# Perceiver cross-attention on one core: value-side context blocks turned by DMA, probability sums on VectorE

## The chip, the cores and the metric

One Trainium2 chip, one core of it. The time is device microseconds of one execution of the whole program. Engines are named as in the profile: PE (TensorE), DVE (VectorE), ACT (ScalarE), POOL (GpSimd), SP (the queue that issues the DMAs).

## The reference, cut to what matters

The program computes one layer: cross-attention of 128 query rows on 12544 context rows, then a chunk of linear attention and a feed-forward block with ternary weights. Nearly all the time, and the whole change, is in the cross-attention.

```python
q = (inputs_q @ Wq).reshape(b, sq, H, HD) * (1.0 / np.sqrt(HD))     # 128 x 16 heads x 128
k = (inputs_kv @ Wk).reshape(b, skv, H, HD)                         # 12544 context rows of 512
v = (inputs_kv @ Wv).reshape(b, skv, H, HD)
scores = jnp.einsum('bqhd,bkhd->bhqk', q, k)
attn = jax.nn.softmax(scores, axis=-1)
ctx = jnp.einsum('bhqk,bkhd->bqhd', attn, v).reshape(b, sq, H * HD)
return ctx @ Wo
```

## The kernel before

**Absorbed weights.** Keys and values are never formed. For each head the query is multiplied by Wk, so that scores are products of a 128x512 query with the context itself; the weighted sum of context rows is multiplied by Wv and Wo at the end.

**Pairs of heads and a Strassen form.** Two heads and two halves of a context block make a 2x2 block product, which is done with seven products (Winograd's form). Operands therefore come in seven blocks, three or four given ones and four sums: A11, A12, A22, S1 to S4 for queries and probabilities, B11, B21, B22, T1 to T4 for the context. Each operand is split into a high and a low float16 part, and three of the four cross products are taken (`product` L1207, `value_product` L1218).

**Steps.** The context is 49 blocks of 256 rows. One step (`make_steps` L49, 136 of them) takes one pair of heads and a window of three neighbouring blocks (128 score columns for each block and head; narrower windows at either end). Eight pairs take turns while the window moves, so a block enters the ring about every 2.8 steps. The ring has 4 slots.

**Two copies of each block.** `make_loads` (L71) orders two loads for each block: kind 0, transposed (features on partitions, in `bulk`, moved through the scores), and kind 1, natural (rows on partitions, in `nring`, moved through the values). Each is four DMAs into the single buffer `stage` (L448, L452), four sums by POOL (`sum_t`, L561), a high part by ACT (`split_hi`, L629 or L632) and a low part by DVE (`split_lo`, L857 or L861). In steps 8 to 130 about three steps in four carry one of them. The transposed ring is laid out so that almost every window is one access pattern; slots 0 and half pieces interleave (`PLACES`, `window` L93). In windows {0,1,2} and {1,2,3} the columns come in another order, so that an exponential is made of two instructions for each head (`split_exp`, L648 and L651), otherwise of one (L655).

**A step on each engine**, in the order of its own queue:
- PE (`step`, `values`): seven score products, six matmuls each (L1214), into four PSUM regions; the last waits for `d_done` from DVE. Then the seven value products of the step two before it (L1227; `LAG` is 2): V1, V5, V6 and its neighbour, V7, V3, and the last, which waits for `vd_done`, the value sum of DVE. 42 score and 63 value matmuls for a full window.
- ACT: copies of partial scores (L686, L690, L692), the split if any, exponential of head 0 (L655 or L648 and L651), copy of V1 (L672), exponential of head 1, copies of V5 and V6 (L677, L681), two alphas (L711), then the high parts of the probabilities (L666): blocks A22, A11, A12 in one, then S1, S3, S2, S4.
- POOL: the four context sums if any, then the four sums of probabilities (`sum_p`, L580).
- DVE: maximum of head 0 (L874), adding and maximum (L869) twice, running row sums (L903, L905), the negated maxima (L881, L883), the split if any, in steps 50 to 112 every second time a quantisation of feed-forward weights (L935, L937, L941), the value sum (`value_sum_d`, L924), five low parts (L892), another value sum (L929), two accumulations (L914).
- SP: for the step before, two DMA transposes of the probabilities from `pp` to `pt` (24 and 18 tiles of 128x128, L462), then context loads, query weights (first steps), feed-forward weights.

An all-reduce over partitions on POOL (L591) stands in step 43, between its sums.

Of the kernel before, what the change touches and what calls it, by code (L numbers as in the profile page):

```python
# [5 lines left out]
P = 128  # L6
D = 512
KC = D // P
# [19 lines left out]
HALF = P // 2  # L28
PLACES = ((0, 1), (2, 5), (3, 4), (6, 7))
TW = P * RING  # L30
# [40 lines left out]
def make_loads():  # L71

    order = sorted([(user(c, False), 0, c) for c in range(NCH)] + [(user(c, False) + LAG, 1, c) for c in range(NCH)])
    loads, at = [], -1
    for need, kind, c in order:
        free = user(c - RING, True) + 1 + LAG * kind if c >= RING else -1
        at = max(free, min(at + 1, need - 1)) if c >= 1 else -1
        assert at < need, (kind, c, free, at, need)  # L80
        loads.append((kind, c, at))
    return loads


LOADS = make_loads()
LOAD_OF = {(kind, c): j for j, (kind, c, _) in enumerate(LOADS)}

# [5 lines left out]
def window(k):  # L93


    _, a, w = STEPS[k]
    slots = {ring_slot(c) for c in range(a, a + w)}
    return {
        frozenset((0, 1, 2)): (0, 6 * HALF, 1, 6 * HALF, (1, 0, 2), 0),
        frozenset((1, 2, 3)): (2 * HALF, 6 * HALF, 1, 6 * HALF, (1, 2, 3), HALF),  # L100
        frozenset((0, 2, 3)): (0, 3 * HALF, 3, 2 * HALF, (0, 2, 3), None),
        frozenset((0, 1, 3)): (0, 5 * HALF, 2, 3 * HALF, (0, 1, 3), None),
        frozenset((0, 3)): (0, 6 * HALF, 2, 2 * HALF, (0, 3), None),
        frozenset((2, 3)): (3 * HALF, 3 * HALF, 2, 2 * HALF, (2, 3), None),
        frozenset((0,)): (0, 2 * HALF, 1, 2 * HALF, (0,), None),
        frozenset((1,)): (2 * HALF, 3 * HALF, 2, HALF, (1,), None),
        frozenset((2,)): (3 * HALF, 2 * HALF, 1, 2 * HALF, (2,), None),
        frozenset((3,)): (6 * HALF, 2 * HALF, 1, 2 * HALF, (3,), None),
    }[frozenset(slots)]


def perceiver_layer(nc, x_d, ctx_d, qk_d, vo_d, aw_d, wg1_d, wg2_d, w12_d, ld_d, normw_d, b1_d,
                    lng_d, lnb_d, b2_d, ident_d, diff_d, mask_d, out_d):
    es = ExitStack()
    with es:
# [30 lines left out]
        rsum = sb("rsum", 2 * H)  # L146
# [44 lines left out]
        PURE = 4  # L191
# [7 lines left out]
        def runs(t, at, stride, n, m):  # L199

            if n == 1:
                return t[:, at:at + m]
            return t[:, at:at + n * stride].rearrange("p (n s) -> p n s", s=stride)[:, :, 0:m]

        def t_moving(k, lo, blk, c):
            start, stride, n, m, _, _ = window(k)
            return runs(bulk16, ((lo * 7 + blk) * 2 + c) * TW + start, stride, n, m)

# [4 lines left out]
        def n_part(c, lo, blk=0, n=1):  # L213
            at = ((ring_slot(c) * 2 + lo) * 7 + blk) * BLK
            return nring16[:, at:at + n * BLK]
# [16 lines left out]
        def bank_a(k):  # L232
            return ps_s[:, D - cols(k):D]

        def bank_e(k):
            return ps_s[:, D:D + cols(k)]
# [29 lines left out]
        in_ctx = sem("in_ctx")  # L266
        in_pt = [sem(f"in_pt{g}") for g in range(2)]
# [106 lines left out]
        def prep_at(k):  # L374

            for j, (kind, c, at) in enumerate(LOADS):
                if at == k:
                    return j, kind, c
            return None

        def t_ring(c, lo):

            a, b = PLACES[ring_slot(c)]
            ring = bulk16[:, lo * 14 * TW:(lo + 1) * 14 * TW].rearrange("p (b w) -> p b w", w=TW)
            if b == a + 1:
                return [ring[:, :, a * HALF:(a + 2) * HALF]]
            return [ring[:, :, a * HALF:(a + 1) * HALF], ring[:, :, b * HALF:(b + 1) * HALF]]

        def t_stage(j, n):

            blocks = stage[:, 0:7 * BLK].rearrange("p (b w) -> p b w", w=P)
            return [blocks[:, :, i * P // n:(i + 1) * P // n] for i in range(n)]
# [8 lines left out]
        def pp_part(k, lo, blk, n=1):  # L401
            at = p_at(k, blk // PURE, lo, blk % PURE)
# [6 lines left out]
        A21 = -1  # L409

        def prob_of(k, g):
            return prob_part(k, (A21, A11)[g], 2)

# [7 lines left out]

        def split_exp(k):
            return window(k)[5] is not None
# [12 lines left out]
        def _(sp):  # L436
# [5 lines left out]
            def load_ctx(j):  # L442
                kind, c, _ = LOADS[j]
                if j:
                    sp.wait_ge(ctx_lo, j)
                if kind == 0:
                    for n, blk in enumerate((B11, B12, B21, B22)):
                        sp.dma_start(stage[:, blk * BLK:(blk + 1) * BLK].rearrange("p (c n) -> p c n", c=2),  # L448
                                     ctx_d[4 * c + n // 2].rearrange("p (c h n) -> p c h n", c=2, h=2)[:, :, n % 2]).then_inc(in_ctx, 16)
                else:  # L450
# [41 lines left out]
            for k in range(1, NS + 1):  # L492
# [979 lines left out]
```

## Time and profile before

| | us |
|---|---|
| median of 3 runs | 2245.78 (2244.88 to 2248.94) |
| profiled execution, its own time | 2249.19 |
| its span, first to last instruction | 2247.4 |
| PE busy | 2000.4 |
| DVE busy | 1769.5 |
| ACT busy | 1252.2 |
| POOL busy | 1114.8 |
| queue of the DMAs, share of 16 engines | 59.2% |

The page counts an engine as busy while an instruction of it runs; overlapping matmuls count once. Its 40 slices show PE at 0.9 or more from about 170 us to 2060 us and a granted clock of 0.9 to 1.0 there. What decides a step can't be seen in such sums; it is in the order of instructions inside one step, which the timeline shows, and in what an engine waited for.

### The profile page before, as it was taken

How to read it: one execution, taken by the hardware profiler on the slowest of the kernel's cores; microseconds unless marked ns; L12 is line 12 of the kernel's file. 1: busy time of each engine (PE TensorE's matmuls, PEld its weight loads, DVE VectorE, ACT ScalarE, POOL GpSimd, SP SyncE). 2: the span in 40 equal slices, each digit the busy share in tenths (PEclk: the TensorE clock that was granted, in tenths of full speed). 3: DMA queues.
4: the chain of work that ended last, by engine and by line, in shares of the span. 5: the costliest groups of instructions: out<-in, count | busy, mean ns of one | idle time of the engine just before them, and what ended most of it. 6: DMA issues, size and time to landing. Idle time of an engine off the chain costs nothing. (4 is left out here: it accounts for less than half of the span.)

```text
span 2247.4 us, 41557 instructions
## 1 busy us (share of the span) xinstructions
PE 2000.4 (89%) x14730; PEld 1441.7 (64%) x14730; DVE 1769.5 (79%) x3383; ACT 1252.2 (56%) x2801; POOL 1114.8 (50%) x949
## 2 busy tenths in 40 slices
PE   4679999999997998999999898989899899999786
PEld 4557676666665675666666676666666666767552
DVE  4667878887885789798888989898988888786526
ACT  3445666666664655565655655555655555565312
POOL 2334656565563645464655646454646556552001
PEclk7799999999999999999999999999999999999997
DMA  3446666666665566566666566566666565655660
GB/s 117 102 105 126 140 144 141 127 142 135 141 135 104 112 126 134 113 142 121 134 132 128 122 138 133 119 134 123 135 131 129 116 127 117 122 109 104 190 213 5
DMA packets 817967, 284.86 MB, mean 127 GB/s; under 512 B 719936, under 2 KB 803904, under 8 KB 816864
## 3 DMA queue, kind: packets, MB, share of 16 engines
q1 hardware_dynamic: 817760, 282.21, 59.2%
q8 instruction: 117, 1.92, 0.4%
q14 instruction: 90, 0.74, 0.1%
HBM read 97.85 MB, written 4.46 MB: 46 GB/s over the span
## 5 line engine op out<-in xcount | busy, mean ns | idle before, releaser
L580 POOL TENSOR_TENSOR prob<-prob 128x384 f32<-128x384 f32 (+2 forms) x544 | 733.4, 1364 | 866.4 <-ACT prob L655 387.4
L892 DVE SCALAR_TENSOR_TENSOR pp<-prob,pp 128x384 f16<-128x384 f32 (+4 forms) x680 | 665.7, 1041 | 0.0
L1214 PE MATMUL ps_s<-bulk 128*128 128x384 f16 (+2 forms) x3264 | 581.7, 322 | 7.1 <-issue 4.4
L1227 PE MATMUL ps_v<-nring,pt 128*128 128x256 f16 x4704 | 582.5, 273 | 3.0 <-DVE acc L914 1.5
L1214 PE MATMUL ps_t<-bulk 128*128 128x384 f16 (+2 forms) x2448 | 453.3, 322 | 118.2 <-DVE mx L869 88.7
L1227 PE MATMUL ps_w<-nring,pt 128*128 128x256 f16 x3528 | 455.0, 274 | 58.2 <-DVE ps_w L924 34.7
L1227 PEld LDWEIGHTS ps_v<-nring,pt 128*128 128x128 f16 x4704 | 460.7, 98 | 71.5 <-DVE acc L828 2.6
L666 ACT ACTIVATE pp<-prob 128x384 f16<-128x384 f32 (+4 forms) x680 | 394.2, 625 | 164.0 <-POOL prob L580 162.4
L1214 PEld LDWEIGHTS ps_s<-bulk 128*128 128x128 f16 x3264 | 317.5, 99 | 192.3 <-issue 5.6
L561 POOL TENSOR_TENSOR stage<-stage 128x256 f32<-128x256 f32 x392 | 375.0, 957 | 112.0 <-DMA stage<-in_ctx 80.2
L1214 PEld LDWEIGHTS ps_t<-bulk 128*128 128x128 f16 x2448 | 223.8, 98 | 308.9 <-DVE mx L869 123.1
L1227 PEld LDWEIGHTS ps_w<-nring,pt 128*128 128x128 f16 x3528 | 337.6, 98 | 125.3 <-DVE ps_w L924 43.7
L924 DVE TENSOR_TENSOR ps_w<-ps_w,part_e 128x256 f32<-128x256 f32 x136 | 58.5, 430 | 260.5 <-PE ps_w L1227 260.5
L655 ACT ACTIVATE prob<-ps_s,nmax 128x768 f32<-128x768 f32 (+2 forms) x72 | 61.4, 852 | 156.0 <-DVE nmax L883 148.8
L632 ACT ACTIVATE nring<-stage 128x1792 f16<-128x1792 f32 x49 | 83.1, 1696 | 67.5 <-POOL stage L561 67.5
L648 ACT ACTIVATE prob<-ps_s,nmax 128x256 f32<-128x256 f32 x64 | 30.3, 473 | 153.6 <-DVE nmax L883 153.4
L861 DVE SCALAR_TENSOR_TENSOR nring<-stage,nring 128x1792 f16<-128x1792 f32 x49 | 100.5, 2051 | 17.1 <-ACT nring L632 17.1
L692 ACT ACTIVATE part_u<-ps_t 128x384 f32<-128x384 f32 (+2 forms) x136 | 65.0, 478 | 86.0 <-PE ps_t L1214 86.0
L629 ACT ACTIVATE bulk<-stage 128x1792 f16<-128x1792 f32 (+1 forms) x61 | 84.3, 1400 | 49.9 <-POOL stage L561 49.8
L686 ACT ACTIVATE ps_t<-ps_s 128x384 f32<-128x384 f32 (+2 forms) x136 | 62.7, 461 | 87.3 <-PE ps_s L1214 87.3
L857 DVE SCALAR_TENSOR_TENSOR bulk<-stage,bulk 128x1792 f16<-128x1792 f32 (+1 forms) x61 | 109.3, 1809 | 0.4 <-ACT bulk L629 0.4
L869 DVE CUSTOM_DVE_ANT_0 ps_t<-ps_t,part_e 128x384 f32<-128x384 f32 (+2 forms) x136 | 74.0, 544 | 41.6 <-PE ps_t L1214 41.6
(198 smaller groups left out, 1788.3 us busy)
## 6 DMA issues: line engine op xcount, KB each, us to landing
stage<-in_ctx SPq DMA_DIRECT2D x392, 128.0 KB, 2.6
wst<-in_w SPq DMA_DIRECT2D x64, 256.0 KB, 3.2
bulk<-in_vo SPq DMA_DIRECT2D x16, 512.0 KB, 5.6
acc<-in_qk SPq DMA_DIRECT2D x11, 512.0 KB, 5.2
pt<-pp SPq DMA_TRANSPOSE x272, 5.6
tern_d<-wter SPq DMA_DIRECT2D x32, 128.0 KB, 3.1
bulk<-tern_d SPq DMA_DIRECT2D x2, 2048.0 KB, 11.0
nring<-in_aw SPq DMA_DIRECT2D x3, 1024.0 KB, 7.1
```

Source lines behind the costliest of these rows:

```text
L561: nc.gpsimd.tensor_tensor(piece(stage, dst), piece(stage, a), piece(stage, b), ALU.subtract).then_inc(t_sum, 1)
L580: nc.gpsimd.tensor_tensor(prob_part(k, dst), prob_part(k, a), prob_part(k, b), op).then_inc(p_sum, 1)
L629: last = nc.scalar.activation(d, t_stage(j, len(dst))[n], ACT.Copy, scale=CTX_SCALE)
L632: nc.scalar.activation(n_part(c, 0, 0, 7), stage[:, 0:7 * BLK], ACT.Copy, scale=CTX_SCALE).then_inc(ctx_hi, 1)
L666: nc.scalar.activation(pp_part(k, 0, blk, n), prob_part(k, blk, n), ACT.Copy, scale=P_SCALE).then_inc(hi_done, 1)
L692: nc.scalar.activation(part_u[:, 0:cols(k)], bank_b(k), ACT.Copy).then_inc(u_copied, 1)
L857: last = nc.vector.scalar_tensor_tensor(lo[n], t_stage(j, len(hi))[n], CTX_SCALE, hi[n], ALU.mult, ALU.subtract)
L861: nc.vector.scalar_tensor_tensor(n_part(c, 1, 0, 7), stage[:, 0:7 * BLK], CTX_SCALE, n_part(c, 0, 0, 7), ALU.mult, ALU.subtract).then_inc( ...
L869: nc.vector.tensor_tensor_reduce(dst, a, b[:, 0:cols(k)], 1.0, LOWEST, ALU.add, ALU.max, accum_out=mx[:, 2 + g:3 + g]).then_inc(done, 1)
L892: nc.vector.scalar_tensor_tensor(pp_part(k, 1, blk, n), prob_part(k, blk, n), P_SCALE, pp_part(k, 0, blk, n), ALU.mult, ALU.subtract).then ...
L1214: ins = mm(out, q_part(e, qlo, a)[:, c * P:(c + 1) * P], t_moving(k, tlo, b, c), start=(first and c == 0 and qlo == 0 and tlo == 0), stop= ...
L1227: ins = mm(dst, pt[:, tile:tile + P], n_part(c, clo, b), start=(first and n == 0 and plo == 0 and clo == 0), stop=(last and n == w - 1 and ...
```

## The change

- **Natural blocks.** The natural loads, their sums and splits are gone. A block is loaded once, transposed, and split into one ring slot, high and low parts side by side (28 tiles of 128x128). SP then turns the whole slot by one DMA transpose into the natural ring (`turn_n`). It is queued behind the two transposes of the probabilities and a load, two steps after the split. PE's values wait for it (`turned`), and so does ACT before a slot is overwritten.
- **Layout.** Slots of the transposed ring lie one after another. Windows {0,1,3} and {0,2,3} are no single pattern, so each of their score matmuls becomes two, of 128 and 256 columns; the others stay one. Since the columns are in slot order everywhere, one exponential serves each head.
- **Probability sums.** The four sums leave POOL. DVE makes them (`prob_sums`), after the split and the quantisation. Behind them stand the low part of the first three blocks, and only then the value sum that PE's last value product waits for, which stood ahead of all low parts.
- **Small things.** The running row sums move from DVE to POOL, both heads at once in two instructions. The maximum of one head is taken along in the adding instruction, one short operation less. The value products pair blocks in another order, with other signs.
- **Order of splits.** Splits fall in steps 1 to 5, then every two or three steps (45 in steps 8 to 130, none in step 44).

```diff
-def make_loads():
-    order = sorted([(user(c, False), 0, c) for c in range(NCH)] + [(user(c, False) + LAG, 1, c) for c in range(NCH)])
...
+def make_splits():
+    at = [-1 if c == 0 else user(c, False) - 2 if c < RING else user(c - RING, True) + 1 for c in range(NCH)]
...
+    slots = sorted(ring_slot(c) for c in range(a, a + w))
+    if slots == [0, 1, 3]:
+        return slots, ((0, 1, 2), (3, 1, 1))
+    if slots == [0, 2, 3]:
+        return slots, ((0, 1, 1), (2, 1, 2))
+    return slots, ((slots[0], slots[-1] - slots[0] if w == 2 else 1, w),)
...
+            def turn_n(c):
+                sp.wait_ge(ctx_lo, c + 1)
+                if c >= RING:
+                    sp.wait_ge(v4_done, user(c - RING, True) + 1)
+                sp.dma_start_transpose(whole_slot(nring16, c).rearrange("p (t q) -> p t q", q=P),
+                                       whole_slot(bulk16, c)).then_inc(in_nt[c % 2], 16)
...
                 turn_p(k - 1, 0)
                 turn_p(k - 1, 1)
-                for j, (_, _, at) in enumerate(LOADS):
-                    if at == k + 1:
-                        load_ctx(j)
+                for c in range(2, NCH):
+                    if SPLIT_AT[c] == k + 1:
+                        load_ctx(c)
+                for c in range(1, NCH):
+                    if SPLIT_AT[c] == k - 2:
+                        turn_n(c)
...
# POOL
-                    sum_t(found[0])
-                sum_p(k)
+                    sum_t(found)
+                if k:
+                    sums(k - 1)
...
# ACT, exponential
-                if split_exp(k):
-                    ...
+                nc.scalar.activation(prob_of(k, g), scores_of(k, g), ACT.Exp, bias=nmax_of(k, g), scale=EXP_SCALE,
+                                     accum_out=total).then_inc(exp_done[g], 1)
...
# DVE
+            def prob_sums(k):
+                for n, (dst, a, b, op) in enumerate(((S1, V21, V22, ALU.add), (S3, V21, V11, ALU.subtract),
+                                                     (S2, S1, V11, ALU.subtract), (S4, S2, V12, ALU.subtract))):
+                    if n == 0:
+                        v.wait_ge(exp_done[0], k + 1)
...
+                    if n == 1:
+                        v.wait_ge(exp_done[1], k + 1)
+                    if n >= 2:
+                        v.wait_ge(p_sum, 4 * k + n - 1 + (n == 3))
+                    nc.vector.tensor_tensor(prob_part(k, dst), prob_part(k, a), prob_part(k, b), op).then_inc(p_sum, 1)
...
                     quant((k - QUANT_AT) // 2)
+                prob_sums(k)
+                lo_part(k, V22, 3, 1)
                 if k >= LAG:
                     value_sum_d(k - LAG)
-                lo_part(k, A22, 3, 1)
                 lo_part(k, S1, 1, 2)
...
# PE, one score product
                 for c in range(2):
                     for qlo, tlo in ((0, 0), (0, 1), (1, 0)):
-                        ins = mm(out, q_part(e, qlo, a)[:, c * P:(c + 1) * P], t_moving(k, tlo, b, c),
+                        at = 0
+                        for run in window(k)[1]:
+                            n = run[2]
+                            out = dst[:, at:at + n * P]
+                            ins = mm(out if n == 1 else out.rearrange("p (n m) -> p n m", m=P),
+                                     q_part(e, qlo, a)[:, c * P:(c + 1) * P], t_moving(k, run, tlo, b, c),
...
```

## Rows read from the trace of the kernel before

**Rows 1.** The page, part 1: engine, busy us (share), instructions.
```profile
PE 2000.4 (89%) x14730; PEld 1441.7 (64%) x14730; DVE 1769.5 (79%) x3383; ACT 1252.2 (56%) x2801; POOL 1114.8 (50%) x949
```

**Rows 2.** Timeline, PE: start us, us, engine line; first score product of steps 8 and 131.
```profile
177.27 2.11 PE L1214 MATMUL ps_s<-bulk 128*128 128x384 f16 x12
...
2049.83 1.47 PE L1214 MATMUL ps_s<-bulk 128*128 128x256 f16 x12
```

**Rows 3.** Timeline of a short step, 1917.69 to 1931.40.
```profile
1917.69 2.11 PE L1214 MATMUL ps_s<-bulk 128*128 128x384 f16 x12
...
1921.80 0.56 DVE L874 TENSOR_REDUCE mx<-ps_s 128x1 f32<-128x384 f32 x1 [0.43 <-PE ps_s L1214]
...
1924.52 2.13 PE L1227 MATMUL ps_v<-nring,pt 128*128 128x256 f16 x18
...
1928.32 2.80 ACT L666 ACTIVATE pp<-prob 128x1152 f16<-128x1152 f32 x5
...
1929.63 0.43 DVE L924 TENSOR_TENSOR ps_w<-ps_w,part_e 128x256 f32<-128x256 f32 x1 [3.83 <-PE ps_w L1227]
...
1931.40 2.11 PE L1214 MATMUL ps_s<-bulk 128*128 128x384 f16 x12
```

**Rows 4.** Timeline of a long step, 1855.89 to 1865.
```profile
1855.89 0.43 DVE L924 TENSOR_TENSOR ps_w<-ps_w,part_e 128x256 f32<-128x256 f32 x1 [1.98 <-PE ps_w L1227]
1856.23 5.94 DVE L892 SCALAR_TENSOR_TENSOR pp<-prob,pp 128x1152 f16<-128x1152 f32 x5
...
1865.01 1.15 PE L1214 MATMUL ps_t<-bulk 128*128 128x384 f16 x6 [1.06 <-DVE mx L869]
```

**Rows 5.** Low parts: timeline of five in a short step; one alone (min/median/max ns).
```profile
1916.27 3.31 DVE L892 SCALAR_TENSOR_TENSOR pp<-prob,pp 128x1152 f16<-128x1152 f32 x5
...
L892 DVE SCALAR_TENSOR_TENSOR pp<-prob,pp x1: 1343/1343/1343, 922.1 to 922.1; 128x1152 f16<-128x1152 f32 x1
```

**Rows 6.** Groups by line and shape (busy us, mean ns); last, line L561's durations.
```profile
L580 POOL TENSOR_TENSOR prob<-prob 128x384 f32<-128x384 f32 x504 | 704.2, 1414 | 799.9 <-ACT prob L651 361.2 <-ACT prob L655 348.2 <-issue 79.6
...
L666 ACT ACTIVATE pp<-prob 128x1152 f16<-128x1152 f32 x126 | 145.0, 1151 | 0.0
L861 DVE SCALAR_TENSOR_TENSOR nring<-stage,nring 128x1792 f16<-128x1792 f32 x49 | 100.5, 2051 | 17.1 <-ACT nring L632 17.1
...
L561 POOL TENSOR_TENSOR stage<-stage x392: 716/922/1939, 9.6 to 1996.3; 128x256 f32<-128x256 f32 x196
```

**Rows 7.** Timeline: a value sum on DVE, and PE's last value product waiting for it.
```profile
1013.00 0.42 DVE L924 TENSOR_TENSOR ps_w<-ps_w,part_e 128x256 f32<-128x256 f32 x1
...
1013.48 1.16 PE L1227 MATMUL ps_w<-nring,pt 128*128 128x256 f16 x9 [0.90 <-DVE ps_w L924]
```

**Rows 8.** Timeline, PE: two score products of a 128-column step.
```profile
2091.29 0.51 PE L1214 MATMUL ps_t<-bulk 128*128 128x128 f16 x6
2091.63 0.50 PE L1214 MATMUL ps_s<-bulk 128*128 128x128 f16 x6
```

**Rows 9.** DVE: line L937 (min/median/max ns), and a sum with two SBUF inputs.
```profile
L937 DVE TENSOR_SCALAR wst<-wst x32: 426/1106/1112, 822.0 to 1780.8; 128x512 f32<-128x512 f32 x32
...
18.69 0.43 DVE L836 TENSOR_TENSOR acc<-acc 128x256 f32<-128x256 f32 x1
```

**Rows 10.** SP's queue in the short step; DMA issues with median us to landing.
```profile
1918.21 6.46 SPq L462 DMA_TRANSPOSE pt<-pp  x2
...
1924.71 2.80 SPq L448 DMA_DIRECT2D stage<-in_ctx  x4
...
pt<-pp SPq DMA_TRANSPOSE x272, 5.6
```

**Rows 11.** Timeline, PE, step 44.
```profile
732.23 2.08 PE L1227 MATMUL ps_w<-nring,pt 128*128 128x256 f16 x9 [12.14 <-ACT ps_w L672]
```

**Rows 12.** Timeline, PE, step 0.
```profile
37.42 0.82 PE L1214 MATMUL ps_t<-bulk 128*128 128x128 f16 x6 [7.51 <-ACT ps_t L686]
```

More of the change, by code:

```diff
@@ L68, in user @@
     return of[-1] if last else of[0]
-def make_loads():
-    order = sorted([(user(c, False), 0, c) for c in range(NCH)] + [(user(c, False) + LAG, 1, c) for c in range(NCH)])
[L76 to L86, printed above, removed]
+def make_splits():
+    at = [-1 if c == 0 else user(c, False) - 2 if c < RING else user(c - RING, True) + 1 for c in range(NCH)]
+    assert all(b - a >= 2 for a, b in zip(at, at[1:])) and all(user(c, False) - at[c] >= 2 for c in range(1, NCH))
+    return at
+SPLIT_AT = make_splits()
 def ring_slot(c):
@@ L96, in window, with block_in @@
     _, a, w = STEPS[k]
[L97 to L109, printed above, removed]
+    slots = sorted(ring_slot(c) for c in range(a, a + w))
[4 more added lines that the diff above has]
+    return slots, ((slots[0], slots[-1] - slots[0] if w == 2 else 1, w),)
+def block_in(k, slot):
+    _, a, w = STEPS[k]
+    return next(c for c in range(a, a + w) if ring_slot(c) == slot)
 def perceiver_layer(nc, x_d, ctx_d, qk_d, vo_d, aw_d, wg1_d, wg2_d, w12_d, ld_d, normw_d, b1_d,
@@ L190, in perceiver_layer @@
         A22, A11, A12, S1, S2, S3, S4 = range(7)
-        PURE = 4
+        V22, V12, V11 = range(3)
+        V21 = -1
+        GROUP = 4
         def slot(k, n=1):
@@ L197, in h_rows_t, with t_moving, t_part, whole_slot @@
             return prob[:, n * D // 2:(n + 1) * D // 2].bitcast(BF16)
-        def runs(t, at, stride, n, m):
+        def t_moving(k, run, lo, blk, c):
+            first, stride, n = run
+            at = first * SLOT + ((lo * 7 + blk) * 2 + c) * P
             if n == 1:
[L202 to L207, printed above, removed]
+                return bulk16[:, at:at + P]
+            return bulk16[:, at:at + n * stride * SLOT].rearrange("p (n s) -> p n s", s=stride * SLOT)[:, :, 0:P]
+        def t_part(c, lo):
+            at = ring_slot(c) * SLOT + lo * 7 * BLK
+            return bulk16[:, at:at + 7 * BLK]
+        def whole_slot(ring, c):
+            return ring[:, ring_slot(c) * SLOT:(ring_slot(c) + 1) * SLOT]
         def q_part(e, lo, blk=0, n=1):
@@ L266, in perceiver_layer @@
         in_ctx = sem("in_ctx")
+        in_nt = [sem(f"in_nt{g}") for g in range(2)]
         in_pt = [sem(f"in_pt{g}") for g in range(2)]
@@ L374, in prep_at, with turned @@
         def prep_at(k):
[L376 to L392, printed above, removed]
+            return next((c for c in range(NCH) if SPLIT_AT[c] == k), None)
+        def turned(engine, c):
+            engine.wait_ge(in_nt[c % 2], 16 * (c // 2 + 1))
         def p_at(k, g, lo=0, blk=0):
@@ L553, in piece @@
                 return t[:, n * BLK:(n + 1) * BLK]
-            sums = [0]
+            sums_t = [0]
             def sum_t(j):
@@ L948, in step @@
                 add_and_max(k, 1)
-                if k:
-                    sums(k - 1)
                 v.wait_ge(s3_done, k + 1)
@@ L997, in _ @@
                 step(k)
-            sums(NS - 1)
             v.wait_ge(lo_done, 5 * NS)
@@ L1233, in values @@
                 pe.wait_ge(in_pt[0], 16 * (k + 1))
-                pe.wait_ge(ctx_lo, max(LOAD_OF[(1, c)] for c in range(lowest, lowest + w)) + 1)
+                for c in range(max(lowest, lowest + w - 2), lowest + w):
+                    turned(pe, c)
                 if k:
@@ L1260, in step @@
                     pe.wait_ge(exp_done[0], k)
-                pe.wait_ge(ctx_lo, max(LOAD_OF[(0, c)] for c in range(a, a + w)) + 1)
+                pe.wait_ge(ctx_lo, a + w)
                 ii = k + 2
@@ L1303, in finish @@
                 for c in range(KC):
-                    last = mm(ps_t[:, (f % 2) * D:(f % 2) * D + HD], w[:, c * HD:(c + 1) * HD],
+                    half = (c + 2) % KC
+                    last = mm(ps_t[:, (f % 2) * D:(f % 2) * D + HD], w[:, half * HD:(half + 1) * HD],
                               ut[:, (f % 2) * D + c * P:(f % 2) * D + (c + 1) * P], start=(c == 0), stop=(c == KC - 1))
```

207 lines of the change are left out of this document (79 added, 128 removed).

## Prediction, made before the changed kernel ran

> **What bounds the kernel now.** I read the page's busy times first: PE 2000.4 us (89%), DVE 1769.5 us (79%) of a 2247.4 us span [rows 1]. Two engines this full may take turns, so I went to the timeline of TensorE and took the start of each step's first score product. Step 8 starts at 177.27 and step 131 at 2049.83: 123 steps in 1872.6 us, 15.22 us each. The shortest steps are well under that, 13.71 us from 1917.69 to 1931.40 [rows 2, 3]. The loop is decided by what makes the others long.
>
> A long step is a loop between DVE and PE. DVE adds the value sum (L924) at 1855.89, after standing idle 1.98 us for PE; only then come the five low parts of the probabilities (L892), 5.94 us; two accumulations and the next maxima follow, and PE waits 1.06 us for that DVE work at 1865.01 [rows 4]. In the short step the same five take 3.31 us [rows 5]. The difference is GpSimd (POOL), whose sums of probabilities take 1.41 us each and 704.2 us in all [rows 6]. Where POOL is quiet a 384-wide low part occupies about 0.47 us, where POOL is at work over 1 us. The Trainium skill (SBUF — State Buffer, Who interferes with whom) says that a VectorE instruction with two SBUF inputs and a GpSimd instruction that reads SBUF exclude each other for a whole instruction. By that rule, the trace agrees: the 3.31 and the 5.94 us are for the same five instructions.
>
> The short step is PE alone: 42 score matmuls from 1917.69 to 1924.52, 63 value matmuls to 1931.40, no wait [rows 3].
>
> **The change, part by part.** The sum is made on steps 8 to 130, measured at 1872.6 us.
>
> *A new floor under each step.* Today the value sum stands before the low parts on DVE; afterwards it stands behind the four sums of probabilities and the low part of the first three blocks. TensorE's last value product waits for it. I walk the short step again, in us from its first matmul. ScalarE (ACT) begins the high part of the three blocks at 10.63 (1928.32), and cannot begin earlier, as the copy before it awaits a value product that PE has not finished sooner; it takes 1.15, so ends at 11.78 [rows 3, 6]. By then DVE has done the four sums: it is idle for 3.83 us before 1929.63 [rows 3], and they need 4 x 0.47 plus waits for their inputs, about 2 us. The low part of 1152 columns takes 1.34 undisturbed [rows 5], of which about 0.07 overlaps the next instruction: the value sum starts at 11.78 + 0.05 + 1.27 = 13.10. PE starts its product 0.48 after that sum's start (1013.00 to 1013.48) [rows 7], so at 13.58, where it now starts at 12.73. Nine matmuls of 0.109 (6.88/63) end the step at 14.56 [rows 3]. So every quiet step grows from 13.71 to 14.56, and no step can be shorter: the wait removed is replaced by one on the same engine in another place. 123 x 14.56 = 1790.9.
>
> *Score products in two runs.* For slots {0,1,3} and {0,2,3} a 384-column matmul becomes one of 256 and one of 128. Pitches: 6.83/42 = 0.1626 us for 384 and 0.109 for 256 [rows 3]; for 128, six in 0.34, 0.0567 [rows 8]. Extra 0.0031 x 42 = 0.13 us a step, and in this stretch 59 steps have such windows: +7.7. The weight load comes twice, but at 128 columns each matmul has its own load already, and the pitch holds it.
>
> *Splitting the context.* Of two splits per block one goes, with its POOL sums (half of 392) and its ACT and DVE halves (2.05 us on DVE [rows 6]). The 45 that stay in this stretch lie on DVE at 8.0 to 9.9 of their step, push the four sums to about 11.9 and the low part by 0.1: +4 (45 x 0.1). In the step before each, POOL's four context sums arrive when the load lands, near 10.9, next to the low part. If POOL gets in first, DVE waits up to a whole such sum, 0.72 to 0.92 [rows 6]. I take half of that, 0.45: 45 x 0.45 = +21; bounds 0 and, with DVE's overrun reaching the next step's maxima (0.5), 45 x 1.4 = 63.
>
> *Weight quantisation.* Three DVE operations in every second step of a stretch; the middle one has a median of 1.11 us and a least of 0.43 [rows 9]. Alone in their place they fit into DVE's idle time. In the 8 steps that also split, they take 1.6 more: the split ends at 9.9, the three at 11.5, the four sums at 13.5 instead of 11.8: +14 (8 x 1.7). Bounds 0 and 20.
>
> *The four sums on DVE*, 128x384, two SBUF inputs: not in the trace of before on this engine. A 256-wide one is 0.43 [rows 9], a 384-wide low part about 0.47 in pitch [rows 5]; I take 0.47. At twice that they would end at 13, past the high part: +1.2 a step; I see no reason for it with POOL quiet. One exponential for two, and one maximum operation less, free ACT and DVE by 0.2 us each, ahead of waits that PE sets: nothing.
>
> *Turning context by DMA.* 28 tiles for each of 49 blocks. The two transposes of a step, 42 tiles, hold SP's queue for 6.46 us [rows 10], so 28 tiles take 4.3. A loop of SP with transposes (6.46), a load (2.80) and a turn (4.3) is 13.6 us, under 14.56, and most loops are shorter. Landing takes 5.6 us [rows 10]; the probabilities of a step are wanted two steps later, their buffer about 11 us later, the turned block a step or more later. Cost nothing, covered by that slack; if the turn pushed the next transposes by more than 4 us, ACT's high parts would wait for them.
>
> *The all-reduce.* In step 44 PE stands still for 12.14 us [rows 11]: ACT holds a copy behind a split whose POOL sums wait behind the all-reduce. Afterwards no split falls in step 44, and the wait goes. In my sum that step is an ordinary one, so this gain is in it.
>
> *The ends.* Step 0 loses its wait of 7.51 us, a split queued ahead of a copy on ACT [rows 12]; steps 3 and 4 have a turn (4.3 us) ahead of the query weight loads that PE waits for: about even, bounds -8 and +10. The narrow last steps get the late value sum too: +2.
>
> Sum: 1790.9 + 7.7 + 4 + 21 + 14 = 1837.6, 35.0 less than 1872.6; with the tail 33 less. The profiled execution took 2249.2 (span 2247.4), 3.4 over the median; it would take 2216, and the median of 2245.8 becomes 2213.
>
> **The rivals.**
> *Slower: POOL's context sums keep colliding.* They land beside the late low parts in 45 steps. At the difference of rows 4 and 5, 5.94 - 3.31 = 2.6 us, of which DVE has 1.5 of slack (by the walk its accumulations end at 2.6 of the next step, and the first maximum is due at 4.11 [rows 3]), plus a whole sum ahead of the first low part, a load step loses about 1.9 instead of 0.45: 45 x 1.45 = 65 more, 2278. With a milder 1.3 each it is 2251. It decides from 45 x 1.2: then nothing is left of the gain. For it: POOL starts on landing, and lost time on DVE now always stands beside POOL. Against: half the context sums and all the large ones are gone, and the load may land behind the low part. The rule on whole-instruction exclusion named above speaks for this rival in each collision; it gives no other size.
>
> *No new wait.* If the value sum came in time after all (high parts earlier than I read), steps would be 13.8: 123 x 13.8 = 1697 + 7.7 + 10, about 155 less, 2090. Against it: the order on DVE is written out and each duration has its row.
>
> *The gain is eaten by the queue.* SP's loop at over 14.6 us where load, turn and weight transfers meet, in about 40 steps: 1 us each gives 2253.
>
> **How the numbers follow.** My case (one new wait, some collisions) 0.63, centre 2213, own range 2180 to 2240. Collisions 0.20, 2245 to 2280. Queue 0.09, about 2253. No wait 0.08, 2090. Low end: 21 + 4 less for collisions, 8 less at the start: 2180. High end 2262, through most of the queue case and the milder part of the collisions. Leaving out 2090 and the worst collisions is 0.2. This kernel's measurement tells about 0.2% from no change, 4.5 us: faster (under 2241.3) 0.67, within 0.12, slower (over 2250.3) 0.21.
>
> **What would show it.** PE: a wait for the value sum on the last value product in nearly every step, near 0.85 us, and steps at 14.6 instead of alternating between 13.7 and 15.5. DVE busy under 1650 us with low parts at 0.47 pitch, POOL's busy under 250 us. No 12 us stop. PE busy up by under 10 us. Wrong if DVE's sums take far over 0.55 us, if the wait on the value sum is missing, or if ACT's high parts wait for transposes.

## The result, and the profile of the changed kernel

The changed kernel takes 2174.53 us (median of 4 runs, 2170.53 to 2179.44), beside 2245.33 us (2243.28 to 2248.94) for the kernel before: ratio 0.9675, interval 0.966 to 0.9691. That is 70.8 us less. The forecast was 33 less and 2213; the measured time lies below its range (2180 to 2262). The profiled execution took 2175.8 us, 73.4 less than that of before; the working below is made on it.

The page of after, part 1, answers rows 1:

```profile
PE 1984.7 (91%) x17330; PEld 1594.6 (73%) x17334; DVE 1660.5 (76%) x3346; ACT 1137.6 (52%) x2484; POOL 294.5 (14%) x465
```

Timeline of TensorE, after, first score products of step 8 and of step 131; it answers rows 2 and 11. The two lines between them are the ends of steps 43 and 44:

```profile
153.98 2.11 PE L1176 MATMUL ps_s<-bulk 128*128 128x384 f16 x12
...
680.47 1.16 PE L1191 MATMUL ps_w<-nring,pt 128*128 128x256 f16 x9 [0.85 <-DVE ps_w L887]
...
695.10 1.16 PE L1191 MATMUL ps_w<-nring,pt 128*128 128x256 f16 x9 [0.76 <-DVE ps_w L887]
...
1975.00 1.26 PE L1176 MATMUL ps_s<-bulk 128*128 128x256 f16 x10
```

Steps 8 to 130 take 1821.0 us where they took 1872.6 [rows 2]. Step 44, with its stop of 12.14 us [rows 11], took 29.1 us and is now one of 14.6. The spans differ by 73.5 us: 51.5 of it in this loop, 20.4 in the first eight steps (148.8 to 128.4) and 2.9 ahead of step 0; from step 131 on, after is 1.4 longer (1.0 shorter in the last steps, 2.4 longer behind them).

Timeline of a quiet step of after (129), from 1945.88 to 1960.44; it answers rows 3:

```profile
1945.88 2.11 PE L1176 MATMUL ps_s<-bulk 128*128 128x384 f16 x12
1946.12 6.39 SPq L443 DMA_TRANSPOSE pt<-pp  x2
...
1952.70 2.13 PE L1191 MATMUL ps_v<-nring,pt 128*128 128x256 f16 x18
...
1953.87 0.56 DVE L863 TENSOR_TENSOR prob<-prob 128x384 f32<-128x384 f32 x1
...
1955.19 1.62 DVE L863 TENSOR_TENSOR prob<-prob 128x384 f32<-128x384 f32 x3 [0.76 <-ACT prob L620]
...
1956.51 2.80 ACT L631 ACTIVATE pp<-prob 128x1152 f16<-128x1152 f32 x5
...
1957.69 1.36 DVE L868 SCALAR_TENSOR_TENSOR pp<-prob,pp 128x1152 f16<-128x1152 f32 x1 [0.88 <-ACT pp L631]
1958.96 0.43 DVE L887 TENSOR_TENSOR ps_w<-ps_w,part_e 128x256 f32<-128x256 f32 x1
1959.30 1.48 DVE L868 SCALAR_TENSOR_TENSOR pp<-prob,pp 128x384 f16<-128x384 f32 x3
1959.44 1.16 PE L1191 MATMUL ps_w<-nring,pt 128*128 128x256 f16 x9 [0.68 <-DVE ps_w L887]
```

In us from the step's start: high part 10.63, low part 11.81, value sum 13.08, TensorE's last value product 13.56, end 14.56. DVE waits 0.88 for the high part, its four sums long done. It is the chain of the forecast (13.10, 13.58, 14.56).

What TensorE waited for, after (total us, times, longest), then the same of before:

```profile
PE ps_w L1191 <- DVE ps_w L887: 117.6, 134, 4.1
```

```profile
PE ps_t L1214 <- DVE mx L869: 88.7, 88, 1.5
...
PE ps_w L1227 <- DVE ps_w L924: 34.7, 31, 2.7
```

A wait for the maxima in 88 steps has gone, and one for the value sum has come in 134 of 136. Of the 123 steps, 102 lie between 14.5 and 14.8 us; before, 34 were under 14.5 and 79 over 14.8.

Groups of after by line and shape (busy us, mean ns; idle before); they answer rows 5 and 6:

```profile
L868 DVE SCALAR_TENSOR_TENSOR pp<-prob,pp 128x384 f16<-128x384 f32 x510 | 325.0, 697 | 2.3 <-ACT pp L631 2.3
L863 DVE TENSOR_TENSOR prob<-prob 128x384 f32<-128x384 f32 x504 | 263.6, 555 | 46.3 <-ACT prob L620 42.0
...
L544 POOL TENSOR_TENSOR stage<-stage 128x256 f32<-128x256 f32 x196 | 197.0, 1005 | 809.9 <-DMA stage<-in_ctx 798.4
L868 DVE SCALAR_TENSOR_TENSOR pp<-prob,pp 128x1152 f16<-128x1152 f32 x126 | 175.6, 1393 | 58.2 <-ACT pp L631 58.1
```

The low parts of 1152 columns are nearly undisturbed (1393 ns against 1343 [rows 5]). Those of 384 aren't. Timeline of after, end of a step with a context load (34, from 534.94 to 549.50), which answers rows 4 and 10:

```profile
546.75 1.36 DVE L868 SCALAR_TENSOR_TENSOR pp<-prob,pp 128x1152 f16<-128x1152 f32 x1 [0.88 <-ACT pp L631]
546.94 4.75 POOL L544 TENSOR_TENSOR stage<-stage 128x256 f32<-128x256 f32 x4 [15.22 <-DMA stage<-in_ctx]
548.02 0.43 DVE L887 TENSOR_TENSOR ps_w<-ps_w,part_e 128x256 f32<-128x256 f32 x1
548.36 3.74 DVE L868 SCALAR_TENSOR_TENSOR pp<-prob,pp 128x384 f16<-128x384 f32 x4
548.51 1.16 PE L1191 MATMUL ps_w<-nring,pt 128*128 128x256 f16 x9 [0.68 <-DVE ps_w L887]
```

The load has landed at 12.0 of the step, 0.2 us behind the start of DVE's long low part. DVE has the long one in 1.36 us, POOL's first waits it out, and only the four of 384 behind the value sum run slowly: 3.74 us where the quiet step has 1.95. PE waits 0.68 us for the value sum, as without a load.

### The profile page after: what moved, and what is told of

Its sections match the earlier page's. It is cut to its first block, busy times and chain, and to the rows that moved or that the text cites. A ratio compares the mean times of both kernels' runs of the same rounds, so it can differ in the third digit from the quotient of the medians.

```text
span 2173.9 us, 46145 instructions
## 1 busy us (share of the span) xinstructions
PE 1984.7 (91%) x17330; PEld 1594.6 (73%) x17334; DVE 1660.5 (76%) x3346; ACT 1137.6 (52%) x2484; POOL 294.5 (14%) x465
## 4 chain that ended last, share of the span: by engine, by line
PE 63%; DVE 19%; issue 8%; ACT 6%; DMA 2%; ACTq 1%; SPq 0%; POOL 0%; DVEq 0%; POOLq 0%
PE ps_s L1176 23%; PE ps_t L1176 18%; PE ps_w L1191 11%; PE ps_v L1191 7%; DVE bulk L817 4%; ACT pp L631 4%; DVE prob L863 4%; DVE pp L868 3%; DVE ps_w L887 2%; DVE mx L833 1%; DMA bulk<-in_vo 1%; PE ps_w L1150 1%; ACT alpha L676 1%; PE ps_v L1163 1%; PE ps_t L1270 1%
## 5 line engine op out<-in xcount | busy, mean ns | idle before, releaser
L1176 PE MATMUL ps_s<-bulk 128*128 128x128 f16 (+2 forms) x4752 | 589.0, 274 | 2.9 <-DVE bulk L809 2.7
L868 DVE SCALAR_TENSOR_TENSOR pp<-prob,pp 128x384 f16<-128x384 f32 (+4 forms) x680 | 515.3, 806 | 62.8 <-ACT pp L631 62.7
L1176 PEld LDWEIGHTS ps_s<-bulk 128*128 128x128 f16 x4752 | 408.4, 99 | 117.3 <-DVE bulk L809 2.9
L1176 PE MATMUL ps_t<-bulk 128*128 128x384 f16 (+2 forms) x3564 | 453.5, 272 | 13.9 <-ACT ps_t L651 13.4
L1176 PEld LDWEIGHTS ps_t<-bulk 128*128 128x128 f16 x3564 | 302.2, 98 | 105.0 <-ACT ps_t L651 14.6
L863 DVE TENSOR_TENSOR prob<-prob 128x384 f32<-128x384 f32 (+2 forms) x544 | 276.0, 540 | 49.8 <-ACT prob L620 44.7
L544 POOL TENSOR_TENSOR stage<-stage 128x256 f32<-128x256 f32 x196 | 197.0, 1005 | 809.9 <-DMA stage<-in_ctx 798.4
L833 DVE TENSOR_REDUCE mx<-ps_s 128x1 f32<-128x384 f32 (+2 forms) x136 | 73.4, 540 | 134.0 <-PE ps_s L1176 134.0
L620 ACT ACTIVATE prob<-ps_t,nmax 128x768 f32<-128x768 f32 (+2 forms) x136 | 118.4, 871 | 0.2
L828 DVE CUSTOM_DVE_ANT_0 ps_s<-ps_s,part_u,mx 128x384 f32<-128x384 f32 (+2 forms) x136 | 82.9, 610 | 46.1 <-PE ps_s L1176 46.1
L877 DVE SCALAR_TENSOR_TENSOR acc<-acc,alpha,ps_v 128x512 f32<-128x512 f32 x128 | 95.7, 748 | 4.5
```

What stands on the lines that cost most here:

```text
L544: nc.gpsimd.tensor_tensor(piece(stage, dst), piece(stage, a), piece(stage, b), ALU.subtract).then_inc(t_sum, 1)
L620: nc.scalar.activation(prob_of(k, g), scores_of(k, g), ACT.Exp, bias=nmax_of(k, g), scale=EXP_SCALE, accum_out=total).then_inc(exp_done[g], 1)
L828: nc.vector.tensor_tensor_reduce(dst, a, b[:, 0:cols(k)], 1.0, (mx[:, 0:1], LOWEST)[g], ALU.add, ALU.max, accum_out=mx[:, 2 + g:3 + g]).th ...
L833: nc.vector.reduce_max(mx[:, g:g + 1], (bank_a, bank_b)[g](k), AX.X).then_inc(mx_done, 1)
L863: nc.vector.tensor_tensor(prob_part(k, dst), prob_part(k, a), prob_part(k, b), op).then_inc(p_sum, 1)
L868: nc.vector.scalar_tensor_tensor(pp_part(k, 1, blk, n), prob_part(k, blk, n), P_SCALE, pp_part(k, 0, blk, n), ALU.mult, ALU.subtract).then ...
```

## The experiments

Theory at their outset: the late value sum sets every step; the gain comes from POOL and DVE no longer working beside each other. The rival: the natural blocks' loads and splits were the cost, and the order on DVE is harmless. In the edits, `prob_sums` makes the four sums of probabilities, `lo_part` a low part and `value_sum_d` the value sum, all on DVE.

**e1: the value sum back in front of the low parts.**

```diff
                 prob_sums(k)
-                lo_part(k, V22, 3, 1)
                 if k >= LAG:
                     value_sum_d(k - LAG)
+                lo_part(k, V22, 3, 1)
```

> The changed kernel with the value sum of DVE put between the four probability sums and the first low part. My theory (the place of the value sum is the floor of 14.56 us under each step): PE's wait for it, 119 us in the changed kernel's trace, falls under 25 us, quiet steps become 13.7 to 13.8 us, and 123 steps save about 0.9 us each: 2174 - 110 = 2064 us, 2050 to 2085. Rival (something else stands right behind, SP's queue of transposes, loads and turns at about 13.6 us in a full loop, or the high parts of ACT): PE waits elsewhere, quiet steps stay over 14.2 us, 2120 us or more.

Measured: 2086.69 us, ratio to the kernel before 0.9268 (0.9246 to 0.9291; all ratios below are to that kernel on the same chip), 88 less than the changed kernel. Steps 8 to 130 take 1734.6 us; 78 of 123 are 13.7 or 13.8 us. So the late place costs 88 us, over half of the gain that the rest of the change brings. It isn't the 2064 us I expected, and just over the range (2050 to 2085): all 45 steps with a split are longer, 37 of them at 14.1 to 14.7 us and the eight that also quantise at 15.3 to 15.7. (These come back below, with e8 and e11.)

**e2 and e10: the kernel before with its natural blocks, probability sums on DVE.** In e2 the value sum stands late, as in the changed kernel; in e10 it stands first.

```diff
-                sum_p(k)                       # POOL
...
+                prob_sums(k)                   # DVE
+                lo_part(k, A22, 3, 1)          # e2; in e10 behind the value sum
                 if k >= LAG:
                     value_sum_d(k - LAG)
-                lo_part(k, A22, 3, 1)
```

> The kernel before with only one part of the change: the four probability sums on DVE, in the changed kernel's order (value sum behind the first low part); natural blocks still loaded, summed and split. If the sums on POOL were what made steps long: steps at 14.6 to 14.9 us in place of 13.7 to 17.5, step 44 still near 29 us, the first eight steps as before (149 us): 2245 - 35 = 2210 us, 2195 to 2220. If the natural blocks were the larger cost: 2230 us or more. If the start was shortened by the sums leaving POOL: first eight steps near 130 us and the time under 2195 us.

> The kernel before with the probability sums on DVE and the value sum right behind them, ahead of the low parts; natural blocks still loaded and split, so a split in about three steps of four. By the theory that a split on DVE ahead of the value sum costs 0.9 us a step: quiet steps 13.7 us, split steps 14.6 to 14.9, steps with quantisation and split 1 us more: 2245 - 65 = 2180 us, 2165 to 2195. If removing the natural blocks were worth nothing beside the order on DVE: near the 2087 us of the turned kernel with that order.

Measured: e2 2232.31 us, 0.9924 (0.9897 to 0.9952); e10 2129.00 us, 0.9472 (0.9442 to 0.9502). What TensorE waited for, e2 and then e10:

```profile
PE ps_w L1243 <- DVE ps_w L939: 147.2, 134, 4.1
```

```profile
PE ps_w L1243 <- DVE ps_w L939: 32.8, 31, 3.3
PE ps_t L1230 <- DVE mx L868: 25.0, 41, 1.1
```

With the natural blocks too, the late place costs 103 us (2232.3 against 2129.0). e2 is 22 us over what I expected, e10 51 under it: moving the sums off POOL is worth 116 us by itself where the value sum stands first, and 13 where it doesn't. Step 44 alone gives about 13 of either. I had expected it to stay near 29 us in e2, as it keeps both its natural split and the all-reduce; it takes 16.2 us there and 16.1 in e10. So the stop of the kernel before also needed the probability sums on POOL.

**e3: the changed kernel with the sums back on POOL and the value sum first.**

```diff
+                sum_p(k)                       # POOL, behind sums(k - 1)
...
-                prob_sums(k)                   # DVE
-                lo_part(k, V22, 3, 1)
                 if k >= LAG:
                     value_sum_d(k - LAG)
+                lo_part(k, V22, 3, 1)
```

> The changed kernel with one part undone: the four probability sums back on POOL, and with them the value sum ahead of all low parts, as before; natural blocks still turned by DMA. Theory (POOL's sums beside the low parts make only those steps long in which POOL also has context sums): 78 steps near 13.8 us, 45 near 15.5 us, steps with quantisation 1 us more, no long step 44, first eight steps near 130 us because few splits fall there: 2150 us, 2135 to 2170, no slower than the changed kernel. Rival (moving the sums off POOL is the source of the gain): 2200 us or more.

Measured: 2111.11 us, 0.9382 (0.936 to 0.9403), 39 under what I expected. Without natural blocks, the sums on POOL cost 24 us (against e1), not 116. The all-reduce is dear here again: POOL begins the probability sums of step 44 only at 676.94 us, after that step's end (676.13), and step 45 takes 19.61 us. Together:

| value sum | sums on | natural blocks loaded (us) | turned by DMA, with the rest of the change (us) |
|---|---|---|---|
| first | POOL | 2245.3 (before) | 2111.1 (e3) |
| first | DVE | 2129.0 (e10) | 2086.7 (e1) |
| late | DVE | 2232.3 (e2) | 2174.5 (after) |

Alone the two helpful parts are worth 134 and 116 us, together 159, so they pay in good part for the same thing. The place of the value sum then takes 88 back. Neither the theory nor the rival holds alone. The 134 us belong to more than the natural blocks: the right column also has the single exponentials, the running row sums on POOL, the shorter maxima, the other order of splits and the two runs, and no run takes these apart. That the shared part is POOL's work beside DVE is my reading; e11 below shows such a meeting for the context sums that are left. (The medians are from several chips; taken from the ratios, these differences shift by up to 5 us.)

**e5: the context load issued between the two transposes of the probabilities.**

```diff
                 turn_p(k - 1, 0)
-                turn_p(k - 1, 1)
                 for c in range(2, NCH):
                     if SPLIT_AT[c] == k + 1:
                         load_ctx(c)
+                turn_p(k - 1, 1)
```

> The changed kernel with the context load put between the two transposes of the probabilities in SP's queue, about 2.7 us earlier, so that POOL's four context sums begin near 9.5 us of a step and lie beside DVE's probability sums and first low part, as I had taken it for the prediction. If each collision costs what I put on it (0.45 us) : 45 x 0.45 = 20 us more than the changed kernel, 2195 us; by the slower rival of the prediction (1.9 us each) 2260 us. If DVE has enough slack for them: within 5 us of 2174.

Measured: 2209.03 us, 0.9822 (0.9792 to 0.9853), 34.5 over the changed kernel. Timeline of e5, the same step 34, from 539.79:

```profile
548.69 3.73 POOL L544 TENSOR_TENSOR stage<-stage 128x256 f32<-128x256 f32 x4 [12.13 <-DMA stage<-in_ctx]
549.09 2.74 DVE L863 TENSOR_TENSOR prob<-prob 128x384 f32<-128x384 f32 x3 [0.76 <-ACT prob L620]
...
551.75 1.88 DVE L868 SCALAR_TENSOR_TENSOR pp<-prob,pp 128x1152 f16<-128x1152 f32 x1
...
554.03 1.16 PE L1191 MATMUL ps_w<-nring,pt 128*128 128x256 f16 x9 [1.36 <-DVE ps_w L887]
```

The load now lands at 8.9 of the step. Three sums take 2.74 us instead of 1.62, the long low part starts 0.15 later and takes 1.88 instead of 1.36, and PE waits 1.36 us instead of 0.68. That is the collision of the forecast at about its price: the 28 steps in the loop with a load and no quantisation lose 13.7 us, 0.5 each. The other 16 steps with a load also quantise, and lose 21.2 us, 1.3 each, which neither forecast had. There the quantisation pushes DVE's sums fully beside those of POOL. Timeline of e5, step 58, from 901.73:

```profile
911.11 3.56 DVE L863 TENSOR_TENSOR prob<-prob 128x384 f32<-128x384 f32 x4
911.22 4.02 POOL L544 TENSOR_TENSOR stage<-stage 128x256 f32<-128x256 f32 x4 [12.72 <-DMA stage<-in_ctx]
...
916.87 1.16 PE L1191 MATMUL ps_w<-nring,pt 128*128 128x256 f16 x9 [2.15 <-DVE ps_w L887]
```

In the changed kernel little of this happens, because the load lands later than I took it to.

**e8: e1 with DVE's low part of a context block cut in two, around the sums.** This asked whether e1's 14.6 us steps are long because the split delays DVE's value sum.

```diff
-                split_lo(k)
...
+                        split_lo(k, 0)         # columns 0 to 895, after the first sum
...
+                split_lo(k, 1)                 # columns 896 to 1791, before the value sum
```

> The kernel with the value sum first, and the low part of a context split cut in two halves on DVE: one behind the first probability sum, while DVE waits for the second exponential (0.76 us in the trace), one behind the fourth sum, while it waits for the value product. If the 14.62 us of the 45 steps with a split are the split's 2 us ahead of the value sum: those steps fall to 13.8 us, 2087 - 37 = 2050 us, 2040 to 2062. Rival (SP's queue or the DMA engines bind in those steps as well): no less than 2075 us.

Measured: 2085.03 us, 0.9271 (0.9247 to 0.9294): no difference from e1, so that explanation fell. Timeline of e8, a split step (35, from 530.28) and the end of the one before:

```profile
528.62 4.52 POOL L544 TENSOR_TENSOR stage<-stage 128x256 f32<-128x256 f32 x4 [14.41 <-DMA stage<-in_ctx]
528.86 5.17 DVE L876 SCALAR_TENSOR_TENSOR pp<-prob,pp 128x1152 f16<-128x1152 f32 x5
...
535.72 0.55 DVE L840 TENSOR_REDUCE mx<-ps_s 128x1 f32<-128x384 f32 x1
...
536.86 1.16 PE L1184 MATMUL ps_t<-bulk 128*128 128x128 f16 x12 [0.48 <-DVE mx L835]
```

PE waits before DVE's split has even begun (it starts at 539.48). What is late is the maximum, behind low parts of the step before that take 5.17 us beside POOL's context sums.

**e11 and e12: POOL's context sums held until DVE's low parts are done**, in e1 and in the changed kernel.

```diff
                 if found is not None:
+                    if k:
+                        pool.wait_ge(lo_done, 5 * k)
                     sum_t(found)
```

> The value-sum-first kernel with one more change: GpSimd holds its four context sums until VectorE's last low part of the step before (wait for lo_done at 5k). Theory: the 14.62 us split steps come from the low parts of the step before, which run at a pitch of 1.0 instead of 0.47 us beside these sums and push the maxima late by 0.8 to 0.9 us. Held, the sums run from about 1.8 to 5.4, ScalarE's high part of the block ends near 7.2, just at the first exponential. Split steps near 13.9, and the step behind 13.8: 45 x 0.75 = 34 less, 2053 us (2043 to 2068). Rival: the split steps are long for their own work (high part on ScalarE and low part on VectorE); held sums then change nothing or make it worse: 2083 or more, split steps 14.6 or more.

> The changed kernel with the same hold alone. Theory: here the value sum's place sets 14.56 us for every step whatever the low parts do, so that the collision of GpSimd's sums with the low parts is covered: 2172 us (2164 to 2180), low parts on average near 0.6 instead of 0.81 us. Rival: the collisions cost here what the forecast put on them, 0.45 us in each of 45 steps: 2155 us or less.

Measured: e11 2046.34 us (2042.38 to 2047.39), 0.9108 (0.9067 to 0.915), 40 less than e1 (36 by the ratios); e12 2170.57 us, 0.9667 (0.9631 to 0.9703), no difference from the changed kernel. Timeline of e1, from the end of step 34 into step 35 (528.92), and, in the fence behind it, the total of this wait (us, times, longest):

```profile
527.50 5.35 DVE L868 SCALAR_TENSOR_TENSOR pp<-prob,pp 128x1152 f16<-128x1152 f32 x5
527.65 4.78 POOL L544 TENSOR_TENSOR stage<-stage 128x256 f32<-128x256 f32 x4 [14.80 <-DMA stage<-in_ctx]
...
535.68 1.16 PE L1176 MATMUL ps_t<-bulk 128*128 128x128 f16 x12 [0.66 <-DVE mx L828]
```

```profile
PE ps_t L1176 <- DVE mx L828: 29.2, 49, 1.0
```

The same place of e11 (step 35 from 520.96), then, in fences of their own, its group of 384-wide low parts, and the durations of its context sums (min/median/max ns):

```profile
519.54 3.22 DVE L870 SCALAR_TENSOR_TENSOR pp<-prob,pp 128x1152 f16<-128x1152 f32 x5
...
522.89 3.15 POOL L544 TENSOR_TENSOR stage<-stage 128x256 f32<-128x256 f32 x4 [18.00 <-DVE pp L870]
...
526.07 1.70 ACT L611 ACTIVATE bulk<-stage 128x1792 f16<-128x1792 f32 x1 [1.45 <-POOL stage L544]
...
526.90 1.15 PE L1178 MATMUL ps_t<-bulk 128*128 128x128 f16 x12
```

```profile
L870 DVE SCALAR_TENSOR_TENSOR pp<-prob,pp 128x384 f16<-128x384 f32 x510 | 249.9, 551 | 0.0
```

```profile
L544 POOL TENSOR_TENSOR stage<-stage x196: 722/727/2440, 9.3 to 1771.6; 128x256 f32<-128x256 f32 x196
```

Apart, both are fast: five low parts in 3.22 us instead of 5.35, four context sums in 3.15 instead of 4.78, and PE's waits for the maximum are down from 29.2 us in all to 2.2. 115 of 123 steps are at 13.7 or 13.8 us, TensorE's own length; the other eight split and quantise, and take 14.7 to 14.8. The loop takes 1699.6. e12's low parts of 384 are as fast (550 ns), and its steps stay at 14.6: there the value sum's place covers it. Its loop is 3.0 us shorter than that of the changed kernel (1818.0): that is about what the collisions cost there, and hardly more than the spread of executions. e11 is the best version found, 9% under the kernel before and 6% under the changed one.

**e4: context blocks 2 and 3 split in steps 2 and 3 instead of later**, one run, on the start.

```diff
+    at[2], at[3] = 2, 3
-    assert all(b - a >= 2 for a, b in zip(at, at[1:])) and ...
```

> The changed kernel with blocks 2 and 3 split in steps 2 and 3 instead of 3 and 6, so that splits stand close together at the start again. If the start (128 us for the first eight steps against 149 before) was shortened because a context load that waits for a split no longer stands ahead of the query weights in SP's queue: steps 1 to 4 grow by 5 to 15 us together. If not, the first eight steps stay within 3 us of 128.

Measured: 2176.84 us. The first eight steps take 129.8 us instead of 128.4. But steps 1 to 4 take 73.5 instead of 67.8, 5.7 more, with step 2 alone 4.7 longer, and steps 5 to 7 give 4.5 back. So both signs of the forecast came, and the run doesn't decide between them: closer splits do delay the early steps (TensorE waits 3.6 us for query weights instead of 1.7), but they move the start as a whole by 1.4 us, so that the positions of the early splits don't explain its gain of 20.

**e6: the kernel before with its all-reduce replaced by a small POOL addition**, one run. It leaves out the sum over partitions, so each partition's weight scale comes from its own rows.

```diff
-                    nc.gpsimd.partition_all_reduce(wsc[:, 2:4], wsc[:, 0:2], P, ...ReduceOp.add).then_inc(w_all, 1)
+                    nc.gpsimd.tensor_tensor(wsc[:, 2:4], wsc[:, 0:2], wsc[:, 0:2], ALU.add).then_inc(w_all, 1)
```

> The kernel before with the all-reduce over partitions replaced by a small POOL addition; the scale of the ternary weights is then not summed over the partitions, so this part of the computation is left out. If the all-reduce made step 44 long: that step 15 us instead of 29, everything else equal, about 14 us less in all, 2231 us. If something else did: step 44 stays over 25 us.

Measured: 2244.53 us in one run, beside a median of 2247.83. In its profile step 44 takes 15.0 us instead of 29.1, but the loop as a whole is only 8 shorter (1864.5). One execution with a profile doesn't separate this from the spread of steps elsewhere; that the stop needs the all-reduce is shown (and, by e2, the probability sums on POOL as well), that removing it is worth its full 14 us isn't.

## Why the prediction was right or wrong, point by point

**The floor of 14.56: right.** Value sum forecast at 13.10, measured 13.08; product 13.58, 13.56; step 14.56, 14.56. e1 shows it from the other side: with the sum in front, quiet steps are 13.70.

**Two runs per score matmul: right, smaller.** Such steps are 14.66, 0.10 more and not 0.13: 59 x 0.10 = 5.9 instead of 7.7.

**Splits on DVE: right.** 0.08 a step against 0.1.

**Quantisation with a split: right, slightly low.** Those steps take 16.0 to 17.0, and some neighbours are longer: about 17 against 14.

**The four sums on DVE: a little dearer, at no cost.** 555 ns each, 0.51 to 0.53 in pitch; they end 0.85 us ahead of the high part in the quiet step shown.

**POOL's context sums: the failed term in the loop.** I put 0.45 us on each of 45 steps, +21, with the landing at 10.9 of the step. It cost 3: the other terms, as measured, leave about that for it (1821.0 less 1790.9 for the floor, 5.9 for the runs, 3.6 for the splits, 17.2 for the quantisation), and e12, which takes the meetings away, has a loop 3.0 shorter. The step that failed is the landing time, which I gave without its working. Rows 10, read through, have the load issued from 7.02 to 9.82 of the short step; a load of the changed kernel lands a median of 2.9 us after its issue, which makes 12 or later. In the changed kernel SP's transposes begin at +0.24 to +0.29 in 108 of the 123 steps, mostly on the wait for a value product of TensorE (L440), and POOL's first context sum comes at 11.3 to 13.4, in 34 of 45 behind the start of the long low part at 11.8 or 11.9. e5 shows that with an earlier landing, at 8.7 to 11.0, the term would have been real, 34.5 us, though over half of it in the steps that also quantise; e11 shows that the collision still takes place, with the 384-wide low parts, and costs 40 us once the value sum's place covers it no more; e12 shows it covered. So the forecast had the mechanism and put it where it doesn't decide.

**The start: the failed term outside the loop.** I took it as even, bounds -8 and +10; it is 23 us shorter. Some 2 to 3 us of this can be spread: e6, whose program is that of the kernel before until step 43, begins step 0 at 26.32 instead of 28.45 and takes 151.4 instead of 148.8 for the first eight steps. Timeline and waits of TensorE, after; they answer rows 12:

```profile
28.90 0.82 PE L1176 MATMUL ps_t<-bulk 128*128 128x128 f16 x6 [1.90 <-ACT ps_t L651]
```

```profile
PE ps_w L1150 <- DMA acc<-in_qk: 1.7, 1, 1.7
```

The stop in step 0 shrinks from 7.51 to 1.90, and its step from 20.3 to 10.4 us (a second stop, 3.74 at its end, is gone too). The first of these gains I had; against it I set turns ahead of the query weight loads, and that cost is the step that failed. No such wait grew. The waits of the kernel before show what I should have read:

```profile
PE ps_w L1190 <- DMA acc<-in_qk: 11.2, 4, 5.6
PE ps_w L1190 <- DMA wst<-in_qk: 3.0, 1, 3.0
```

TensorE stood 14.2 us for query weights before and 1.7 after. On SP these stood behind context loads, mostly natural ones, that wait for a split to free `stage`; in the changed kernel the weights are in time although a turn of 4.2 to 5.3 us stands ahead of some. I priced the queue's new entry, and not the removed one.

That the natural loads have to go for this isn't shown: e2 and e10 keep them, and there TensorE waits 3.9 and 4.8 us for query weights. Nor does this wait make the start: their first eight steps still take 145.8 and 141.5 us, against 126.6 in e3, with turned blocks and a wait of 1.8. Most of the 20 us thus comes with the turned blocks and what goes with them, half of it in step 0. Another part is the clock: in step 4, 6.8 us shorter, the mean granted clock is 0.93 where it was 0.77 (a mix of the two levels, 1.2 and 2.4 GHz), and the same products keep TensorE busy for 12.3 us instead of 15.8. What makes up the rest is open.

I also misread where the early splits fall: not "steps 1 to 5" but 1, 3, 6, 8 and 11. The count of 45 in the loop and none in step 44 was right, and by e4 these positions move the start as a whole by 1.4 us.

**The turn by DMA costs nothing: right.** PE waits for no turned block in the loop. The all-reduce: right for its step (14.6 us), but for a cause that is only part of it: with the split kept in step 44 and the sums on DVE (e2, e10) that step is at 16 us already. By e6 one shouldn't count its stop as gain in full.

**The forecasts for the profile.** Low parts at a 0.47 pitch, DVE under 1650 and POOL under 250 us were wrong (1660.5 and 294.5), all three through the collisions of the 384-wide parts: e11 and e12, which take these away, have DVE at 1583 and 1582, POOL at 236. PE busy up by under 10 us: it fell by 15.7, with the same products. e11 issues the same matmuls as after and shows 1956.2. In the quiet step the wait adds 0.86 us, of which 0.68 shows as idle; the rest counts as busy, because matmuls on both sides of a stop don't overlap. So this number moves with the waits and is no measure of work.

**The rivals.** Queue: no sign. Collisions: wrong for this kernel; in e5, which brings them about, they cost about 0.8 us a load, not 1.9. No new wait, 2090: wrong for this kernel. e1, which takes the wait away, has 2086.7, but that this is so near is luck: its loop is 20 us longer than the rival's 1715 (1697 + 7.7 + 10), and its start over 20 shorter.

In sum: the forecast gain of 33 became 73.4 in the profiled execution. 23 of the difference is the start, 16.5 the loop, and about 1 what follows. The mechanism of the loop, one new wait in each step, was right; the steps that failed are the cost of the collisions (21, measured 3) and the cost of the turns ahead of the query weights (taken to cancel the gain of step 0; no such wait showed). In the loop the quantisation, 3 too low, hid a little of the first.

## What to carry to other kernels

When work moves between engines, find what then ends a step, and look at the order on that engine before crediting the gain: here one line's place took back 88 of 159 us. A collision of two engines has a place in the step, so work out when the transfer that starts it lands, from the wait that its own queue obeys after the change; then ask whether anything behind it decides. For a shared queue, list what is removed from ahead of each remaining entry as carefully as what is added.

## What the hardware showed that was not expected

- A VectorE low part and a GpSimd sum that meet take turns: in e1 a 384-wide low part goes from a pitch of 0.47 to 1.0 us, a 128x256 GpSimd sum from a duration of 0.73 to 0.92 us (alone as e11 shows them). Who is first keeps going: the 1152-wide low part took 1.36 us with POOL waiting behind it, and 1.88 where POOL was there first. The Trainium skill (SBUF — State Buffer, Who interferes with whom) has this as a lock held for a whole instruction. The trace agrees in that each waits for the other; but a low part and a sum together take 1.0 us, not the 1.2 of 0.47 and 0.73 added, so the turns are a little shorter than the whole instructions.
- It catches small instructions too. Timeline of e3, then the durations of the same one-column maximum in the changed kernel (min/median/max ns): with two SBUF inputs it takes 0.98 us beside a sum on POOL, and has a median of 0.16 us otherwise.

```profile
543.01 0.99 POOL L577 TENSOR_TENSOR prob<-prob 128x384 f32<-128x384 f32 x1 [4.34 <-issue]
543.04 0.98 DVE L858 TENSOR_TENSOR mx<-mx 128x1 f32<-128x1 f32 x1
```

```profile
L841 DVE TENSOR_TENSOR mx<-mx x136: 158/160/481, 35.5 to 2018.2; 128x1 f32<-128x1 f32 x136
```
